# The first three feed-forward layers on fp16 parts, their bounds found on chip, and x^T loaded two pairs at a time

## What is computed

```python
# x: 32 x 256 tokens of 128; memory: 4096 slots of 128; hidden width 512
q = x @ Wq.T + bq
probs = softmax(q @ memory_keys.T / sqrt(128))
x = layernorm(x + (probs @ memory_values) @ Wo.T + bo)
h = silu((x @ w1.T) * s1) * ((x @ w2.T) * s2)
h = gelu((h @ h1.T) * s_h1)
h = gelu((h @ h2.T) * s_h2)
x = layernorm(x + (h @ w3.T) * s3)
```

## Time and profile before

| | us |
|---|---|
| median of 3 runs (1116.14 to 1117.8) | 1117.59 |
| the profiled execution | 1117.46 |
| its span | 1115.5 |

### The profile page before, as it was taken

How to read it: one execution, slowest core, us unless ns; L and a number is a source line. 1 busy time by engine, 2 the same in 40 slices (tenths; PEclk the granted TensorE clock), 3 DMA queues, 4 the chain that set the end, 5 groups by cost and what they waited for, 6 DMA issues and landing times.

```text
span 1115.5 us, 20017 instructions
## 1 busy us (share of the span) xinstructions
PE 1079.3 (97%) x5324; PEld 770.6 (69%) x5324; DVE 972.2 (87%) x1806; ACT 903.1 (81%) x1609; POOL 643.0 (58%) x617
## 2 busy tenths in 40 slices
PE   6899999999999999999999999979999999999996
PEld 5666666666666666666666666646888888888875
DVE  6999999999999999999999899897888887888884
ACT  6787788878887888888878878788788888888883
POOL 0487888888888888888888888760211211121111
PEclk9999999999999999999999999999999999999998
DMA  6879888988988889888888998891010010011000
GB/s 202 203 185 212 198 201 210 209 200 202 209 203 206 203 207 210 200 202 209 206 203 204 212 200 188 193 255 55 12 46 28 28 56 28 28 35 50 11 13 27
DMA packets 83957, 165.89 MB, mean 149 GB/s; under 512 B 19664, under 2 KB 47824, under 8 KB 83792
## 3 DMA queue, kind: packets, MB, share of 16 engines
q1 hardware_dynamic: 71536, 154.29, 58.7%
q10 hardware_dynamic: 12384, 11.16, 3.5%
HBM read 22.76 MB, written 8.39 MB: 28 GB/s over the span
## 4 chain that ended last, share of the span: by engine, by line
PE 42%; SPq 13%; issue 11%; POOL 10%; ACT 10%; DMA 6%; DVE 5%; ACTq 1%; POOLq 0%; DVEq 0%
PE ring L1090 13%; SPq L380 12%; PE ring L1091 12%; POOL pT L549 10%; DMA slot_p<-rows 6%; ACT rows L629 5%; ACT pT L638 4%; PE o_ps L1017 2%; PE s_ps L1045 2%; PE s_ps L1043 2%; PE s_ps L1044 2%; PE o_ps L1020 2%; PE o_ps L1022 2%; DVE rows L795 2%; DVE rows L828 1%
## 5 line engine op out<-in xcount | busy, mean ns | idle before, releaser
L549 POOL TENSOR_TENSOR pT<-slot_p,pT 128x512 f16<-128x512 f32 x482 | 546.0, 1167 | 124.4 <-ACT pT L638 124.3
L638 ACT ACTIVATE pT<-slot_p 128x512 f16<-128x512 f32 x512 | 296.5, 617 | 73.8 <-DMA slot_p<-rows 68.6
L828 DVE TENSOR_SCALAR_CACHE_REDUCE rows<-s_ps 128x1024 f32<-128x1024 f32 x256 | 309.4, 1209 | 40.5 <-DMA slot_p<-rows 19.9
L795 DVE STREAM_TRANSPOSE rows<-rows 128x1024 f32<-128x1024 f32 x256 | 316.9, 1239 | 5.9 <-issue 4.1
L629 ACT ACTIVATE rows<-rows,bias 128x1024 f32<-128x1024 f32 x256 | 291.6, 1139 | 6.4 <-DVE bias L836 5.9
L1043 PE MATMUL s_ps<-keys,q_buf 128*128 128x512 f32 x512 | 249.2, 487 | 6.8 <-DVE rows L828 3.5
L1017 PE MATMUL o_ps<-pT,v_hi 128*128 128x512 f16 x512 | 197.4, 385 | 13.3 <-POOL pT L549 6.6
L1045 PE MATMUL s_ps<-keys,q_buf 128*128 128x512 f32 x512 | 202.4, 395 | 0.0
L1044 PE MATMUL s_ps<-keys,q_buf 128*128 128x512 f32 x512 | 201.1, 393 | 0.0
L1020 PE MATMUL o_ps<-pT,v_lo 128*128 128x256 f16 x1024 | 196.1, 273 | 0.0
L1022 PE MATMUL o_ps<-pT,v_hi 128*128 128x512 f16 x512 | 194.6, 380 | 0.0
(11 more groups left out here) (110 smaller groups left out, 1329.2 us busy)
## 6 DMA issues: line engine op xcount, KB each, us to landing
slot_p<-rows SPq DMA_DIRECT2D x1024, 128.0 KB, 3.0
x_in<-in_x SPq DMA_DIRECT2D x16, 256.0 KB, 3.4
x_in<-in_xT ACTq DMA_DIRECT2D x30, 128.0 KB, 3.3
out<-y_out SPq DMA_DIRECT2D x15, 256.0 KB, 2.4
o_scratch<-o_sum ACTq DMA_DIRECT2D x29, 128.0 KB, 2.7
o_in<-o_scratch SPq DMA_DIRECT2D x14, 256.0 KB, 3.1
z<-in_w_all ACTq DMA_DIRECT2D x25, 113.0 KB, 2.7
rows<-in_w_all SPq DMA_DIRECT2D x1, 2816.0 KB, 12.1
```

The costliest lines, as they stand in the source:

```text
L549: nc.gpsimd.tensor_tensor(halves(s % RING, 1), slots_first(pp, s), halves(s % RING, 0), ALU.subtract).then_inc(split, 1)
L638: nc.scalar.activation(halves(s % RING, 0), slots_first(pp, s), ACT.Copy).then_inc(highed, 1)
L795: nc.vector.transpose(row_piece(tile, k), row_piece(tile, k)).then_inc(turned, 1)
L828: nc.vector.tensor_scalar(row_piece(tile, k), s_ps[:, j % 2, :], 1.0, None, ALU.mult, ALU.max, accum_out=part_max[:, tile, k:k + 1]).then_ ...
```

## The change

- `w_all` is fp16, and so are the split of x and the parts of the inputs of `h1` and `h2` (`x1_hi`, `x1_lo`, `h_hi[0..1]`, `h_lo[0..1]`). `w3` is copied back to fp32r by ScalarE, and its inputs stay fp32r.
- So that the second gelu's input fits in fp16, the kernel finds bounds for the weights and scales on chip: the weight check now keeps the maximum of the weights as well as of the rest (`find_maxima`), spreads seven maxima over the partitions through TensorE (`turn_maxima`, `spread_maxima`, `share_maxima`, `keep_maxima`), and makes powers of two that go into the scales (`set_scales`, nine operations on VectorE ahead of the split of block 0).
- A check chunk is 256 columns instead of 226. Its load is issued in step 9 instead of step 3, its maximum is taken at piece 2 instead of 3, over 2 x 256 columns.
- The first gelu is computed once to fp32; ScalarE copies it, scaled, to the fp16 high part (`gelu_high`), and VectorE's low part scales it too. After chunk 1 the order is gelu 2, high 1, gelu 3, high 2, high 3.
- Where low weights are not zero, TensorE multiplies in fp32 by raw weights. GpSimd's subtractions for them are gone; in turn 0 GpSimd scales the raw `h2` weights (128 x 2048) whatever the branch.
- `x_in` holds two pairs. In even frames ScalarE loads x^T for pairs f + 2 and f + 3 at once; in odd frames it loads none.
- The load of the raw weights waits for the last scores instead of all sends.

```diff
-CHECK_COLS = 226
+CHECK_COLS = 256
...
-        self.w_all = sb("w_all", [P, CHECK_COLS * CHECKS], FP32R)
+        self.w_all = sb("w_all", [P, CHECK_COLS * CHECKS], FP16)
+        self.w3_hi = sb("w3_hi", [P, HC * P], FP32R)
...
+    def set_scales(self, dve):
+
+        dve.wait_ge(self.bounding, 1)
+        self.nc.vector.tensor_tensor(self.sizes[:, :], self.maxima[:, 1:4], self.maxima[:, 4:7], ALU.mult).then_inc(self.bounding, 1)
...
+        for col, by, factor in ((HC, self.inverses[:, 0:1], 1.0), (2 * HC, self.powers[:, 0:1], 1.0), (3 * HC, self.powers[:, 1:2], 2.0 ** 9)):
+            self.nc.vector.tensor_scalar(self.scales[:, col:col + HC], self.scales[:, col:col + HC], by, factor,
+                                         ALU.mult, ALU.mult).then_inc(self.scales_set, 1)
+        self.nc.vector.tensor_scalar(self.h1_scale[:, :], self.inverses[:, 1:2], 2.0 ** -9, None, ALU.mult).then_inc(self.scales_set, 1)
...
-    x_in = sb("x_in", [P, 2 * P], FP32)
+    x_in = sb("x_in", [P, 2, 2 * P], FP32)
...
-        for tile in range(2):
-            for k in range(PIECES):
-                sp.wait_ge(sent[tile][k], 16 * GROUPS * PAIRS)
+        sp.wait_ge(scored, 8 * PAIRS)
         sp.dma_start(raw, w_raw[:, 0:W_COLS]).then_inc(raw_loaded, 16)
...
+            if is_step(i, 0):
+                pool.wait_ge(raw_loaded, 16)
+                pool.wait_ge(stage.scales_set, 4)
+                nc.gpsimd.tensor_tensor(raw_h2, raw_h2, stage.h1_scale[:, :].broadcast_to([P, HC * HID]), ALU.mult).then_inc(raw_scaled, 1)
...
-                if t == 3 and checking(f):
-                    at_least(act, w_rested, f - FIRST_CHECK)
+                if t == 9 and checking(f):
+                    at_least(act, w_maxed, f - FIRST_CHECK)
                     act.dma_start(w_check, w_raw[:, bass.ds((f - FIRST_CHECK) * CHECK_COLS, CHECK_COLS)]).then_inc(check_loaded, 16)
...
-                if t == 13 and valid(f + 2, PAIRS):
+                if t == 13 and par == 0 and valid(f + 2, PAIRS):
                     act.wait_ge(q_projected, f + 2)
-                    act.dma_start(x_in[:, :], xT[:, bass.ds((f + 2) * 2 * P, 2 * P)]).then_inc(x_loaded, 16)
+                    act.dma_start(x_in[:, :, :], xT[:, bass.ds((f + 2) * 2 * P, 4 * P)]).then_inc(x_loaded, 16)
...
+        def gelu_high(b, j):
+
+            act.wait_ge(gelu_f[0], 4 * b + j + 1)
+            nc.scalar.activation(h_hi[1][:, j, :], gelu[:, 0, j, :], ACT.Copy, scale=stage.h1_scale[:, :]).then_inc(gelu_h[0], 1)
...
-                gelus(i + 1, 1, mid1_done, (mid2_done, 4 * (i + 1)), (1, 2, 3))
+                gelu_high(i + 1, 0)
+                for j in (1, 2, 3):
+                    mid1_of(i + 1, j)
+                    if j >= 2:
+                        gelu_high(i + 1, j - 1)
+                gelu_high(i + 1, 3)
...
-                if j == 3 and checking(f - 1):
+                if j == 2 and checking(f - 1):
                     dve.wait_ge(w_rested, f - FIRST_CHECK)
-                    nc.vector.reduce_max(low_parts[:, bass.ds(f - FIRST_CHECK - 1, 1)], w_rest, AX.X,
+                    nc.vector.reduce_max(low_parts[:, bass.ds((f - FIRST_CHECK - 1) * 2, 2)],
+                                         check_room.rearrange("p (n c) -> p n c", n=2), AX.X,
                                          apply_absolute_value=True).then_inc(w_maxed, 1)
...
                     if j < 2:
-                        at_least(pe, gelu_h[0], 4 * (b - 1) + bank + 1)
+                        at_least(pe, gelu_f[0], 4 * (b - 1) + bank + 1)
```

More of the change, by code:

```diff
@@ L384, in layers @@
     ctx = hold
[L386 to L390, removed]
+    stage.x1_hi, stage.x1_lo = (sb(name, [P, BT], FP16)[:, :] for name in ("x1_hi", "x1_lo"))
+    in_room = sb("in_room", [P, 2, HC, BT], FP16)[:, :, :, :]
+    raw = sb("raw", [P, W_COLS], FP32)[:, :]
+    assert BT + HC * BT + W_COLS == 2 * SLOTS
+    raw_h2 = raw[:, W_AT["h2"]:W_AT["w3"]]
     x1T, x1_hi, x1_lo, scales, table_room = stage.x1T, stage.x1_hi, stage.x1_lo, stage.scales, stage.table_room
@@ L748, in _ @@
                 stage.keep_x1T(act, 0)
+        nc.scalar.activation(stage.w3_hi[:, :], stage.w_all[:, W_AT["w3"]:W_COLS], ACT.Copy).then_inc(stage.w3_ready, 1)
         load_table(ACT.Silu)
@@ L769, in _ @@
         stage.output_half(act, PAIRS - 1, 1)
-        gelus(0, 1, mid1_done, (mid2_done, 0))
+        act.wait_ge(stage.scales_set, 4)
+        for j in range(HC):
+            mid1_of(0, j)
+            gelu_high(0, j)
         turns(act, turn)
@@ L1096, in layer @@
-        def layer(out, name, j, src, sem_done, low_weights, width=HID, parts_ready=None):
-            split_products(out, [(weight(name, k, j, width), weight_low(name, k, j, width),
-                                  h_hi[src][:, k, :], h_lo[src][:, k, :]) for k in range(HC)], sem_done, low_weights,
-                           parts_ready if j == 0 else None)
+                nc.tensor.matmul(out, w, hh, start=n == 0, stop=False)
+                last = nc.tensor.matmul(out, w, hl, start=False, stop=n == len(pairs) - 1)
@@ new lines, in split_products, with whole_products, layer @@
+            last.then_inc(sem_done, 1)
+        def whole_products(out, pairs, sem_done, parts_ready=None):
+            for n, (w, h) in enumerate(pairs):
+                if parts_ready:
+                    pe.wait_ge(parts_ready[0], parts_ready[1] + n + 1)
+                last = nc.tensor.matmul(out, w, h, start=n == 0, stop=n == len(pairs) - 1)
+            last.then_inc(sem_done, 1)
+        def layer(out, b, name, j, src, sem_done, low_weights, width=HID, parts_ready=None):
+            parts_ready = parts_ready if j == 0 else None
+            if low_weights:
+                whole_products(out, [(raw_weight(name, k, j, width), gelu[:, src - 1, k, :] if src else product(b, k))
+                                     for k in range(HC)], sem_done, parts_ready)
+            else:
+                split_products(out, [(weight(name, k, j, width), h_hi[src][:, k, :], h_lo[src][:, k, :])
+                                     for k in range(HC)], sem_done, parts_ready)
```

207 lines of the change are left out of this document (123 added, 84 removed).

## The result

| kernel | median us (range) | ratio to before, 95% interval |
|---|---|---|
| before | 1116.88 (1116.14 to 1117.8) | |
| changed | 1137.26 (1136.31 to 1139.55) | 1.0185 [1.0167, 1.0203] |

The account below looks back on a forecast made before the run. It took TensorE's stream to bound the FFN, and in attention matmuls nearly matched by a 44.5 us ring of sends, landing, ScalarE and GpSimd. From 1117.5, -6.0 + 1.0 + 0.1 + 5.4 = +0.5 gave 1118.0 us, range 1109 to 1124.

Parts of the forecast that it names:

- Part 5: Attention: check load and doubled x^T load just ahead of the last sends cost 0.45 us an even frame, +5.4 us.
- Part 2: Turn 0: GpSimd's 128 x 2048 product makes VectorE's five low parts later, +1.0 us, from 0 to +3.
- Part 3: Bounds on chip: nine small VectorE operations ahead of block 0's split, about 0.2 us each, nearly all covered, +0.1 us.
- Part 1: FFN: fp16 matmuls save 0.96 us a block, ScalarE's extra copy shifts 0.44: -6.0 us, from +6.6 to -15.4.
- (c): FFN: ScalarE's extra copy is hidden and TensorE gets all its 0.96 us a block: 1108.6 us, chance 0.07.
- (d): FFN: fp16 matmuls are no faster than fp32r while ScalarE's shift stays: 1130.6 us, chance 0.03.
- the cover: Block 0: GpSimd's eight steps end at 743.05, VectorE's four low parts at 742.04, so 1 us of delay is covered.
- Part 4: Attention's weight check: load moved from step 3 to 9 shrinks a 0.81 us VectorE wait as its maximum grows: 0.
- frame 28: Attention frame with two added 256 KB loads: sends land in 4.5 us, projections 0.84 us further apart, taken as upper bound.
- rival (a): Attention: the loads don't reach the critical landing of the last sends: 1112.6 us, chance 0.25.
- third place: Waits at a third place, as in frames 28 to 31, would show the forecast wrong altogether; no size given.
- rival (b): Attention: last sends land as late as in frame 28, 0.84 us each even frame, 10 in all: 1122.6 us, chance 0.20.

Follow-up runs that it names:

- t3: Changed kernel with GpSimd's 128 x 2048 product cut into eight of 128 x 256, same place and work: 1129.97 us.
- t1: Changed kernel with GpSimd's 128 x 2048 product run only on the path with low weights: 1134.0 us.
- t2: Changed kernel with the nine scale operations moved from ahead of block 0's split to behind VectorE's four low parts: 1136.37 us.
- e4: Changed kernel with only VectorE's maximum back behind the bias, over the low part alone; a constant replaces the weights' maximum: 1137.84 us.
- b1: Kernel before the change with only the weight check's load moved from step 3 to step 9: 1123.04 us, ratio 1.0058.
- e1: Changed kernel with x^T loaded for one pair in every frame, not two pairs in every even frame: 1129.49 us.
- e3: Changed kernel with one-pair x^T loads, check's load at step 3, maximum over the low part behind the bias, constant for the weights' maximum: 1123.66 us.

## Why the forecast was wrong

The forecast was 1118.0 us, in a range of 1109 to 1124; 1137.26 was measured. Two steps of it failed. Part 5 priced the late landing of the last sends at 0.45 us an even frame, +5.4 in all, and 1.14 an even frame, 12.8 us, came. Parts 2 and 3 priced the transition at +1.1, on the ground that low parts with slack would carry it, and it grew by 8.9, since a norm and a split that TensorE waits for carried it.

**Part 1 (forecast -6.0).** The mechanism was right, a term was mis-sized. fp16 matmuls stand 0.216 us apart as forecast, in `h1` and `h2`, so rivals (c) and (d) fall. The shift on ScalarE was taken as 0.44 from a copy of 0.57 us; the two copies, which now scale by a column, take 1.32, and the shift is 1.93 - 1.28 = 0.65. 0.81 - 0.65 = 0.16 us a block, as measured (21.69 to 21.53). Measured are -2.2 from the first to the last residual sum and -0.5 in the last block; with the fp16 matmuls ahead of the first sum it is about -3 as an estimate, not -6.0. The wait of TensorE's load for VectorE's product, forecast at 0.4, is 0.76.

**Part 2 (forecast +1.0, 0 to 3).** The step that failed: I priced one long product by VectorE's slow-down beside eight short ones of 1.4, and put it on the low parts, which have slack. (Its own length, forecast at 5.7, is 3.60.) But the loser waits for a whole instruction (t3), the product starts 0.13 us ahead of the normalisation TensorE waits for, and behind the wait the clock is at its lower level, a term that the forecast didn't have. Measured 5.9 by t1's transition. The forecast had named the first of these and kept it out of its sum: the Trainium skill (SBUF — State Buffer, Who interferes with whom) says that the loser of the shared port blocks for the whole instruction. By that rule, L203 and the product agree (5.27 us beside a product of 3.60, against 2.01 without, 2.27 with pieces). The page also lists the one-input `tensor_scalar` and `cast` among the VectorE instructions that can contend in a two-port mode, which I had passed over; L203, L281 and L229 are such, and all three stretched.

**Part 3 (forecast +0.1).** The step that failed is the cover. "0.2 us each" is right where GpSimd is idle (1.67 for nine), and they were placed where it is not: 4.6 us. The forecast put them against VectorE's low parts behind the split, and left out that TensorE's first layer waits for the split itself. TensorE was through the values that stand ahead of the first layer by 752.9, and waited for the split until 755.15. The cover named, GpSimd's steps ending later than VectorE's, was itself made in part of the contest between the two: with VectorE's low parts not yet begun GpSimd's eight steps took 9.09 us instead of the 11.37 of the earlier trace rows, and 10.90 in t2, where they meet again. The first layer comes 2.6 us later, and behind this wait too the clock is low (0.51 from 756.0 to 759.3). t2's transition gives 1.6 us back.

**Part 4 (forecast 0).** The cover worked as told: sends beside step 3 now land in 2.3 us instead of 3.4, and VectorE's larger maximum is hidden (e4). But a price of nothing for the move was wrong. What the load joins was left to part 5, for the even frames alone, together with the doubled x^T. Alone it costs 5.8 us (b1; e1 against e3), as much as everything I had put down for part 5, and it costs in the full frames too when an x^T load of 128 KB stands behind it there.

**Part 5 (forecast +5.4, bounds 0 and 0.84 an even frame).** Place and direction were right: the even frames grew and the full ones stayed at 22.08. The size is 1.14 us an even frame, outside the bounds. These came from frame 28 as the heaviest traffic in the trace, but its 4.5 us are a median over 32 sends, not over the last four, and say little on what another load does just there. "Latencies don't add up", the argument for rival (a), fails here: on average 3.6 us before, 3.8 and 3.9 with one load more or the other larger, 4.2 with both. Nor is the landing all of it: it grew by 0.6 us, the even frame by 1.14. A second engine came late: VectorE waits 1.86 us for a late group of sends, at a place where it had not waited, which is the "third place" that the forecast said would make it wrong altogether. No run takes its share from that of ScalarE's wait. Rival (b) had the direction, at 10 of the 12.8 us.

**Sum.** Forecast against measured, by stage: parts 4 and 5 +5.4 and +12.8 (of it 11.2 come back in e3, 1.6 are open); parts 2 and 3 +1.1 and, with part 1's share in it, +8.9 in the transition (t1 takes back 5.9, t2 1.6; the rest wasn't taken apart, and the lower clock lasted longer there than before the change: 0.52 from 747.0 to 752.7, against 0.66 from 734 to 739 before, behind the same wait of 3.39 us); part 1 -6.0 and -2.7 in the rest of the FFN. Together 19.0 by trace. No error offset another: every part came out slower than forecast.

## What to carry to other kernels

Price a moved load at its new place as well as its old one. The dearest place that was tried is just ahead of the transfer that a ring waits for, and the two loads put there cost more than their sum. Where two engines contend, ask how long the longest single instruction of the other one is, and keep long ones away from a short chain on the path. When a cover is named, ask whether it stays as long once the edit has changed what runs beside it.

## What the hardware showed

- A VectorE operation on 128 x 4 numbers takes 0.2 us alone (t2) and about 1.15 beside GpSimd's low parts, which take 9.09 / 8 = 1.14 us each: not bandwidth, but a turn of the other engine.
- It goes the other way too. In the kernel with the later scales (t2) a GpSimd sum that takes 1.26 us elsewhere took 7.94 while VectorE issued a row of operations on SBUF:

```profile
761.88 7.94 POOL L171 TENSOR_TENSOR xb<-x_in,bo_all 128x512 f32<-128x512 f32 x1 [4.40 <-DMA x_in<-in_x]
```

- Waits of TensorE of 4.25 and 2.29 us were each followed by about 3 us at the lower clock. In t1 and t3, where the first of them was 1.0 and 1.2 us, the clock stayed at its upper level. So a wait on the path can cost more than its own length. The length alone doesn't tell how much: a wait of 3.39 us was followed by some 3 us at the lower level in the kernel before and by some 6 in the changed one.
